# A graph network's last norm: finishing a row in its PSUM bank, and releasing the bank with the sum

## Chip, cores and metric

One core of a Trainium2 chip (trn2). The time is the device time of the whole program, in microseconds; lower is better. The engines are PE (matrix products), DVE (vector), ACT (activations), POOL (here it issues the indirect DMAs) and SP (here it issues the plain DMAs).

## What is computed

Two graph layers over 100,000 nodes with 32 features and 50,000 edges sorted by their end node. The first is a spline convolution, the second an attention layer with 8 heads, both with residuals. For this text only the end of the second layer counts:

```
h  = layer_norm(gat_conv(h, edges) + h, g1, be1)
ff = relu(h @ w1 + b1) @ w2 + b2
x  = x + (layer_norm(ff + h, g2, be2))        # (v - mean) * rsqrt(var + eps) * g2 + be2
```

Everything is fp32.

## The kernel before

Nodes are kept as 125 partitions by 800 slots of 32 features. A unit of work is 125 x 512: 16 slots. The centring of the norms is folded into the matrices (`center`), so a product leaves already centred rows in a PSUM bank; what is left of a norm is the square (ACT, `square`, L921), the sum over 32 features (DVE, `spread`, L1231), the root (ACT, L926), the reciprocal (DVE, `scale_of`, L1236) and the product with it.

Stages, as they follow each other in the queue of every engine, written out by hand:

- A, to about 770 us: spline layer; POOL gathers rows of x (L428).
- B, 25 chunks, two half-turns each: POOL scatters the 25 chunks of new rows (L450, released by L1462 of DVE, semaphore `x1_ready`) and gathers the rows for later chunks between them. Beside each chunk, plain nodes ("units") pass through the whole second layer in three steps n1, n2, n3 in successive half-turns. Seven units are started in ten half-turns, at half-turns 0, 1, 3, 4, 6, 7 and 9 (`UNIT_AT`). Edge rows go through steps e1 to e4.
- D, 25 turns: POOL gathers from the new table (L428, `x_table`); three units in five turns, and from turn 13 on the attention sums of two edge blocks.
- E, 25 rows in five blocks: the rows with edges are finished (`y_finish`) and POOL scatters each to the output, 16 indirect DMAs a row (L476).

`finish_rows` ends n3 in B (35 times) and D (15 times) and every row in E (25 times). It reads the bank that `back_product` on PE has filled with the centred sum of the feed-forward and its input.

The C banks: there are two in B and D and one in E (`cq.depth`). PE fills them in turn. Before it fills one it waits until `c_done` has counted the release of the bank's previous use (`cq.room`). In B the order of fills in a half-turn is n2, e3 or e4, n3, e1 or e2, n1, as far as the step is present; in D it is n2, d2, d1, n3, n1, then the sums of x_early. A `step(...)` on DVE is an instruction that signals a semaphore, and a wait for it behind it: the result is in place before the next instruction starts.

```
def product(cols_T, right, n=GF, bias=None, plus=None, t_at=None, frees=None):
    at, bank = cq.next()
    pe.wait_ge(c_done, cq.room)
```

Of the kernel before, what the change touches and what calls it, by code (L numbers as in the profile page):

```python
# [30 lines left out]
N, E, F, H, HID, KS = 100000, 50000, 32, 8, 128, 9  # L31
P = 125
TN = N // P
NB, NJ, CE = 5, 5, 16
# [15 lines left out]
NU, ND = len(UNIT_AT), len(UNIT_AT_D)  # L50
SLOTS = NU + ND
assert NB * SLOTS * CE == TN and SLOTS == 2 * NJ
CREDIT = 4
# [54 lines left out]
def turn(h, first=False, last=False):  # L108

    at = node_stages(UNIT_AT, HALVES, h)  # L110
    for stage, lag in ((("e3", 1), ("e1", 0)) if h % 2 == 0 else (("e4", 1), ("e2", 0))):
        at[stage] = ((h // 2 - lag) % NJ, h // 2 < lag)
    return {stage: (n, back) for stage, (n, back) in at.items() if not (first and back or last and not back)}


def gnn_program(nc, x, src, dst, edge_attr, w0, root_w, root_b, w_gat, att_src, att_dst, bias_gat,
# [10 lines left out]
    with ExitStack() as ctx:  # L127
# [55 lines left out]
        g2_b = sb("g2_b", [128, F]); be2_b = sb("be2_b", [128, F])  # L183
# [67 lines left out]
        unit = lambda t, k: t[0:P, k, :]  # L251
# [885 lines left out]
        def _(dve):  # L1137
            v = nc.vector
            steps = Uses()
            R = NB * P  # L1140
            tq, cq, vq, nq, rq = Uses(2), Uses(2), Uses(4), Uses(), Uses(2)
            slots = lambda a: a.rearrange("p (s f) -> p s f", f=F)
            wide = lambda a: a.unsqueeze(2).to_broadcast([P, CE, F])

            def step(i):

                at, _ = steps.next()
                i.then_inc(dve_step, 1)
                dve.wait_ge(dve_step, at + 1)
# [84 lines left out]
            def scale_of(k, at):  # L1234
                dve.wait_ge(std_ready, at + 1)
                step(v.reciprocal(unit(rstd, k), unit(std, k)))  # L1236

            def bank_ready():
                at, bank = cq.next()
                dve.wait_ge(c_ready, at + 1)  # L1240
                return at, C[bank][0:P, :]
# [8 lines left out]
            def rows_over_std(k, at):  # L1250
                at_c, rows = bank_ready()
                scale_of(k, at)
                v.tensor_tensor(slots(unit(hrow, k)), slots(rows), wide(unit(rstd, k)), ALU.mult).then_inc(c_done, 1)  # L1253
                return at_c
# [124 lines left out]
            for _ in range(0, 2 * NB, 4):  # L1379
                at, _ = tq.next()  # L1380
# [6 lines left out]
            at, _ = tq.next()  # L1387
# [8 lines left out]

            def finish_rows(x1_part, to, at, signal):

                at_c = rows_over_std(3, at)
                v.tensor_tensor(slots(x1_part), slots(x1_part), be2_b[0:P, :].unsqueeze(1).to_broadcast([P, CE, F]), ALU.add)  # L1400
                dve.wait_ge(c_done, at_c + 1 + CREDIT)
                step(v.tensor_tensor(slots(unit(hrow, 3)), slots(unit(hrow, 3)), g2_b[0:P, :].unsqueeze(1).to_broadcast([P, CE, F]), ALU.mult))
                v.tensor_tensor(to, x1_part, unit(hrow, 3), ALU.add).then_inc(signal, 1)  # L1403


            heads_of = lambda a: a[0:P, :].rearrange("p (h t) -> p h t", h=H)
# [59 lines left out]
            for h in range(HALVES):  # L1466
                b_turn(0, turn(h, first=True))
            steps.restart(); cq.restart()
            STEPS = 4 * NU + NJ * (1 + 5 + 1 + 2)
            with dve.Fori(0, NB - 1) as b:  # L1470
                cq.loop(b, B_USES["c"]); nq.loop(b, B_USES["n"]); steps.loop(b, STEPS)
                for h in range(HALVES):
                    b_turn(b + 1, turn(h))
                cq.end(NB - 1, B_USES["c"]); nq.end(NB - 1, B_USES["n"]); steps.end(NB - 1, STEPS)
            for h in range(2):
# [151 lines left out]
            for b in range(NB):  # L1627
                for w in range(NJ):
                    d_turn(b, w, first=b + w == 0)
                    at = b * NJ + w  # L1630
# [147 lines left out]
```

## Time and profile before

| | |
|---|---|
| median of 3 runs | 3327.99 us (3320.49 to 3328.42) |
| the profiled execution | 3314.93 us, its span 3313.1 us |
| PE busy | 2241.8 us (68%) |
| DVE busy | 1858.4 us (56%) |
| ACT busy | 841.2 us (25%) |
| POOL busy | 2543.9 us (77%) |
| mean granted clock of PE | 0.785 |

Busy shares are means over stages with different limits. A line number in a row is the line in the kernel before. "[1.08 <-DVE hrow L1253]" at the end of a row is the time that the engine stood idle before the instruction, and what ended it; "issue" there means that nothing in the profile explains the idle time.

### The profile page before, as it was taken

What the parts mean: (1) busy time and instruction counts of PE and PEld (TensorE: products, weight loads), DVE (VectorE), ACT (ScalarE), POOL (GpSimd) and SP (SyncE); (2) the same over time, 40 slices, a digit from 0 to 9 for tenths busy, and PEclk for the clock granted to TensorE, in tenths of its full rate; (3) what the DMA queues carried; (4) which work ended last, traced back from release to release, by engine and by line L of the source; (5) the groups of instructions that cost most, each with busy time, mean ns of one, the idle gap of its engine ahead of it and who ended that gap; (6) DMA issues with size and microseconds to landing.
All of it is one profiled execution on the core that took longest, in us unless ns stands there. A gap on an engine that the chain in (4) does not pass through costs nothing.

```text
span 3313.1 us, 33504 instructions
## 1 busy us (share of the span) xinstructions
PE 2241.8 (68%) x10666; PEld 1571.2 (47%) x10666; DVE 1858.4 (56%) x3250; ACT 841.2 (25%) x1614; POOL 2543.9 (77%) x2011
## 2 busy tenths in 40 slices
PE   2877777757777777777777645737767557888730
PEld 1554544535555655565555434534444334455420
DVE  4787988894443433434333313347767578989610
ACT  1332222212323232333323212322222212222210
POOL 7788888888787888788888788888883166888877
PEclk9888888877878787887777766767888668888755
DMA  2322232221212111212111111111110101111100
GB/s 58 87 67 67 68 73 69 55 65 26 39 29 39 38 39 32 43 38 42 36 36 29 28 12 31 24 18 28 21 24 9 44 16 23 33 29 32 28 10 10
DMA packets 116212, 123.93 MB, mean 37 GB/s; under 512 B 70726, under 2 KB 72747, under 8 KB 116070
## 3 DMA queue, kind: packets, MB, share of 16 engines
q0 software_dynamic: 64000, 30.57, 9.9%
q1 hardware_dynamic: 52070, 91.52, 8.7%
q8 instruction: 82, 1.34, 0.2%
q14 instruction: 60, 0.49, 0.0%
HBM read 59.51 MB, written 64.00 MB: 37 GB/s over the span
## 4 chain that ended last, share of the span: by engine, by line
POOL 62%; issue 18%; DVE 9%; PE 9%; ACT 1%; DMA 0%; POOLq 0%; DVEq 0%; ACTq 0%
POOL ring L428 38%; POOL x_table L450 15%; POOL out_rows L476 9%; DVE region L1591 2%; PE V L793 2%; PE C L544 2%; PE V L532 1%; DVE region L1583 1%; PE C L508 1%; DVE region L1262 1%; PE T L493 1%; DVE region L1573 1%; DVE var L1231 1%; PE C L538 1%; PE C L540 0%
## 5 line engine op out<-in xcount | busy, mean ns | idle before, releaser
L428 POOL DMA_INDIRECT ring<-in_x,index x800 | 1040.4, 1300 | 244.3 <-issue 244.0
L476 POOL DMA_INDIRECT out_rows<-ring,index_out x400 | 518.8, 1297 | 272.3 <-DVE ring L1403 152.0
L1231 DVE TENSOR_REDUCE var<-sq 125x16 f32<-125x512 f32 x325 | 220.8, 682 | 802.3 <-ACT sq L921 672.1
L428 POOL DMA_INDIRECT ring<-x_table,index x400 | 495.8, 1240 | 127.0 <-issue 127.0
L450 POOL DMA_INDIRECT x_table<-region,index_out x400 | 485.9, 1215 | 121.9 <-issue 121.9
L532 PE MATMUL V<-xT,w_q 128*128 128x500 f32 x600 | 363.3, 756 | 90.0 <-ACT hid L932 56.5
L921 ACT ACTIVATE sq<-C 125x512 f32<-125x512 f32 x300 | 179.2, 598 | 912.3 <-PE C L544 422.7
L544 PEld LDWEIGHTS C<-w_c,hid 128*125 128x125 f32 x2400 | 317.0, 217 | 0.0
L544 PE MATMUL C<-w_c,hid 128*125 128x32 f32 x2400 | 316.0, 295 | 0.0
L508 PE MATMUL C<-center,xT 128*125 128x128 f32 x1400 | 243.8, 333 | 104.6 <-DVE hrow L1253 61.7
L493 PE MATMUL T<-ident,hrow 125*128 125x125 f32 x1000 | 188.9, 326 | 167.6 <-DVE hrow L1247 137.0
L508 PEld LDWEIGHTS C<-center,xT 128*125 128x125 f32 x1400 | 223.3, 239 | 149.2 <-issue 74.1
L532 PEld LDWEIGHTS V<-xT,w_q 128*128 128x128 f32 x600 | 141.7, 251 | 269.5 <-issue 128.5
L566 PE MATMUL V<-region,hT 128*125 128x384 f32 x600 | 254.2, 539 | 18.3 <-DVE region L1326 17.2
L493 PEld LDWEIGHTS T<-ident,hrow 125*128 125x128 f32 x1000 | 143.3, 171 | 210.1 <-DVE hrow L1247 115.7
L913 ACT ACTIVATE hT<-T 128x500 f32<-128x500 f32 x250 | 146.5, 588 | 373.6 <-PE T L493 315.3
L932 ACT ACTIVATE hid<-V,cols 128x500 f32<-128x500 f32 x300 | 190.6, 679 | 102.2 <-PE V L532 96.7
L493 PE MATMUL T<-ident,ring 125*128 125x125 f32 x300 | 60.3, 337 | 223.4 <-DMA ring<-in_x,index 119.9
L1334 DVE TENSOR_REDUCE region<-region 125x128 f32<-125x1152 f32 x100 | 210.9, 2111 | 0.0
L1326 DVE TENSOR_TENSOR region<-V,region 125x384 f32<-125x384 f32 x300 | 155.7, 551 | 74.4 <-PE V L566 63.9
L1591 DVE TENSOR_REDUCE region<-region 125x128 f32<-125x1024 f32 x100 | 187.8, 1898 | 0.0
L793 PE MATMUL V<-gat_bd,hT 128*125 128x512 f32 x280 | 158.8, 700 | 16.4 <-DVE region L1583 13.6
(248 smaller groups left out, 3207.6 us busy)
## 6 DMA issues: line engine op xcount, KB each, us to landing
ring<-in_x,index POOLq DMA_INDIRECT x800
nodes<-in_x SPq DMA_DIRECT2D x25, 500.0 KB
x_table<-nodes SPq DMA_DIRECT2D x25, 500.0 KB
x_plain<-nodes SPq DMA_DIRECT2D x25, 500.0 KB
nodes<-x_plain SPq DMA_DIRECT2D x50, 250.0 KB
out_rows<-nodes SPq DMA_DIRECT2D x50, 250.0 KB
x_table<-region,index_out POOLq DMA_INDIRECT x400
ring<-x_table,index POOLq DMA_INDIRECT x400
```

Of the source, the lines that this page charges most:

```text
L428: pool.indirect_dma_start(out=ring[0:P, j, s * F:(s + 1) * F], out_offset=None, in_=table, in_offset=bass.IndirectOffsetOnAxis(ap=index[0: ...
L450: pool.indirect_dma_start(out=x1_table[:, :], out_offset=bass.IndirectOffsetOnAxis(ap=index_out[0:P, j, s:s + 1], axis=0), in_=rows_out[0: ...
L476: pool.indirect_dma_start(out=out[:, :], out_offset=bass.IndirectOffsetOnAxis(ap=index_out[0:P, j, s:s + 1], axis=0), in_=ring[0:P, j, s * ...
L493: i = nc.tensor.transpose(T[bank][:, g * P:(g + 1) * P], rows[:, g * GF:(g + 1) * GF], ident[0:P, 0:P])
L508: i = mm(C[bank][0:P, g * n:(g + 1) * n], cols_T[:, g * P:(g + 1) * P], right, start=bias is None and plus is None, stop=True, skip_group_ ...
L532: mm(V[4 - fq.depth + bank][:, 0:WT], w1_q[:, t, :], nT, start=True, stop=True).then_inc(f_ready, 1)
L544: i = mm(C[bank][0:P, (4 * g + t) * F:(4 * g + t + 1) * F], hid[:, t, g * P:(g + 1) * P], w2_c[:, :], start=False, stop=True, skip_group_c ...
L566: mm(V[bank][0:P, 0:3 * GF], hT[:, HE[j], g * P:(g + 1) * P], w0_bd[:, q * 3 * GF:(q + 1) * 3 * GF], start=True, stop=True).then_inc(v_rea ...
L793: mm(banks[bank][0:P, :], hT[:, k, g * P:(g + 1) * P], gat_bd[:, q * 512:(q + 1) * 512], start=True, stop=True).then_inc(v_ready, 1)
L1231: v.tensor_reduce(unit(var, k), slots(squares(k)), AX.X, ALU.add).then_inc(var_ready, 1)
L1334: v.tensor_reduce(msgs[0:P, bass.ds(cv * W + g * GF, GF)], products[0:P, (g % 2) * KS * GF:(g % 2 + 1) * KS * GF].rearrange("p (k c) -> p ...
L1591: v.tensor_reduce(diff[0:P, c * W + g * GF:c * W + (g + 1) * GF], weighted[0:P, (g % 2) * H * GF:(g % 2 + 1) * H * GF].rearrange("p (h c) ...
```

## The change

`finish_rows` applies the reciprocal deviation and the weight g2 in place in the C bank, one after the other, and adds the old row from there. The tile `hrow` 3 is no longer written by it. The addition of the bias be2 to the old row comes first. The bank is released by the last sum, no longer by the product with the reciprocal deviation; the signal to SP or POOL (`signal`) is no longer attached to the sum but is given by a separate instruction behind a wait for the sum. The number of steps in a block of the loop is adapted.

```diff
             def finish_rows(x1_part, to, at, signal):
 
-                at_c = rows_over_std(3, at)
+                _, rows = bank_ready()
+                scale_of(3, at)
                 v.tensor_tensor(slots(x1_part), slots(x1_part), be2_b[0:P, :].unsqueeze(1).to_broadcast([P, CE, F]), ALU.add)
-                dve.wait_ge(c_done, at_c + 1 + CREDIT)
-                step(v.tensor_tensor(slots(unit(hrow, 3)), slots(unit(hrow, 3)), g2_b[0:P, :].unsqueeze(1).to_broadcast([P, CE, F]), ALU.mult))
-                v.tensor_tensor(to, x1_part, unit(hrow, 3), ALU.add).then_inc(signal, 1)
+                step(v.tensor_tensor(slots(rows), slots(rows), wide(unit(rstd, 3)), ALU.mult))
+                step(v.tensor_tensor(slots(rows), slots(rows), g2_b[0:P, :].unsqueeze(1).to_broadcast([P, CE, F]), ALU.mult))
+                v.tensor_tensor(to, rows, x1_part, ALU.add).then_inc(c_done, 1)
+                dve.wait_ge(c_done, cq.at + 1 + CREDIT)
+                dve.sem_inc(signal, 1)
...
-            STEPS = 4 * NU + NJ * (1 + 5 + 1 + 2)
+            STEPS = 5 * NU + NJ * (1 + 5 + 1 + 2)
```

## Rows read from the trace of the kernel before

**Rows 1.** The page's chain by engine and costliest group, and POOL's waits (total, times, longest).

```profile
POOL 62%; issue 18%; DVE 9%; PE 9%; ACT 1%; DMA 0%; POOLq 0%; DVEq 0%; ACTq 0%
...
L428 POOL DMA_INDIRECT ring<-in_x,index x800 | 1040.4, 1300 | 244.3 <-issue 244.0
...
POOL out_rows L476 <- DVE ring L1403: 152.0, 5, 115.8
```

**Rows 2.** Windows, stage B: length, busy PE, PEld, DVE, ACT, POOL, clock, DMA, GB/s.

```profile
795.00:1895.00 1100.00, 823.16 (x4140) 627.18 (x4140) 429.88 (x816) 326.76 (x651) 880.33 (x720) 0.80 0.19 36
```

**Rows 3.** Timeline, one half-turn of B: start, duration, engine, line, operation, output, inputs.

```profile
1332.55 1.12 PE L508 MATMUL C<-center,xT 128*125 128x128 f32 x8
...
1335.46 0.69 DVE L1253 TENSOR_TENSOR hrow<-C,rstd 125x512 f32<-125x512 f32 x1
...
1336.29 2.06 PE L508 MATMUL C<-center,xT 128*125 128x128 f32 x8 [2.62 <-DVE hrow L1253]
1336.67 0.68 DVE L1402 TENSOR_TENSOR hrow<-hrow,g_b 125x512 f32<-125x512 f32 x1
...
1337.39 0.69 DVE L1403 TENSOR_TENSOR nodes<-nodes,hrow 125x512 f32<-125x512 f32 x1
1338.00 0.24 DVE L1236 RECIPROCAL rstd<-std 125x16 f32<-125x16 f32 x1
...
1341.18 1.09 PE L493 MATMUL T<-ident,hrow 125*128 125x125 f32 x4 [2.83 <-DVE hrow L1247]
```

**Rows 4.** Timeline, end of B: last chunk ready, first of its scatters.

```profile
1861.69 0.17 DVE L1462 COPY index_out<-scatter_to 125x16 int32 x1
...
1872.31 1.20 POOL L450 DMA_INDIRECT x_table<-region,index_out  x1 [0.30 <-issue]
```

**Rows 5.** Timeline, first finished row of stage E.

```profile
2633.14 0.69 DVE L1403 TENSOR_TENSOR ring<-nodes,hrow 125x512 f32<-125x512 f32 x1
...
2634.80 2.43 POOL L476 DMA_INDIRECT out_rows<-ring,index_out  x1 [115.77 <-DVE ring L1403]
```

**Rows 6.** Timeline, PE: first gathered chunk of D, and the last that it waits for.

```profile
1927.20 1.07 PE L493 MATMUL T<-ident,ring 125*128 125x125 f32 x4 [38.46 <-issue]
...
2197.44 0.65 PE L493 MATMUL T<-ident,ring 125*128 125x125 f32 x4 [1.48 <-DMA ring<-x_table,index]
```

**Rows 7.** Groups by form (mean ns), and one line's instructions (ns min/median/max).

```profile
L1253 DVE TENSOR_TENSOR hrow<-C,rstd 125x512 f32<-125x512 f32 x125 | 86.4, 691 | 4.3
L1402 DVE TENSOR_TENSOR hrow<-hrow,g_b 125x512 f32<-125x512 f32 x75 | 51.4, 685 | 0.0
...
L1403 DVE TENSOR_TENSOR nodes<-nodes,hrow x50: 691/691/766, 796.3 to 2594.3; 125x512 f32<-125x512 f32 x50
```

**Rows 8.** Timeline, first and last n1 product behind an n3, of 19.

```profile
817.03 1.14 PE L508 MATMUL C<-center,xT 128*125 128x128 f32 x8 [1.08 <-DVE hrow L1253]
...
1858.56 0.69 DVE L1253 TENSOR_TENSOR hrow<-C,rstd 125x512 f32<-125x512 f32 x1
...
1859.38 1.58 PE L508 MATMUL C<-center,xT 128*125 128x128 f32 x8
```

**Rows 9.** Timeline, stage D, DVE's first product behind a finish.

```profile
2440.74 0.69 DVE L1583 TENSOR_TENSOR region<-V,region 125x512 f32<-125x512 f32 x1 [0.98 <-PE V L793]
```

**Rows 10.** Timeline, stage E, from POOL's last long stop.

```profile
2803.11 0.69 DVE L1253 TENSOR_TENSOR hrow<-C,rstd 125x512 f32<-125x512 f32 x1
...
2806.65 1.19 POOL L476 DMA_INDIRECT out_rows<-ring,index_out  x1 [20.31 <-DVE ring L1403]
...
2823.24 0.69 DVE L1253 TENSOR_TENSOR hrow<-C,rstd 125x512 f32<-125x512 f32 x1
...
2830.98 1.70 POOL L476 DMA_INDIRECT out_rows<-ring,index_out  x1 [0.30 <-issue]
...
2918.17 0.69 DVE L1403 TENSOR_TENSOR ring<-nodes,hrow 125x512 f32<-125x512 f32 x1
...
2934.89 1.19 POOL L476 DMA_INDIRECT out_rows<-ring,index_out  x1 [0.31 <-issue]
```

## The prediction

> **What bounds the kernel now.** I read the page first. PE, the busiest compute engine by share, and POOL are both far from idle, but the chain that ended last is POOL's for 62% of the span, and nearly all of it is the issuing of indirect DMAs [rows 1]. So the next question is where POOL stands still. The waits of POOL show only five real stops, 152.0 us in all, and all five lie in the last stage, where POOL scatters finished rows and waits for the sum L1403 [rows 1]. Everywhere else it goes from one DMA to the next with 0.3 us between. An edit that touches DVE, the C banks and PE can therefore cost something in two ways: it moves one of these stops, or it makes some stage so late that POOL gets a new stop. For the second the reader has to look at how much time there is between "data ready" and "POOL takes it", stage by stage.
>
> Three stages hold `finish_rows`: stage B (about 768 to 1894 us, 35 finishes), stage D (to 2595, 15) and stage E (from 2597, 25).
>
> Stage B is not paced by POOL. PE has no wait for a gather there, and DVE is busy 430 us of 1100 [rows 2]. It is one long chain that hands a row from PE to ACT to DVE and back, half-turn by half-turn. One half-turn is in [rows 3]: DVE reads the bank of the finished row (L1253, 1335.46), PE waited 2.62 us for exactly that and starts the n1 product 0.83 us later (1336.29), then comes ACT's square, DVE's reduce, the root and the reciprocal, and the next half-turn's transpose at 1341.18, again after a wait of 2.83 us. In the trace each of these links starts within a tenth of a microsecond or so of the end of the one before, plus the time that a signal takes.
>
> **Where B meets POOL.** Each of its 25 chunks ends in L1462, which releases 16 scatters. The last chunk is ready at 1861.69 and its first scatter starts at 1872.31 [rows 4]. DVE to POOL takes some time: L1403 at 2633.14 is written by 2633.83 and the scatter starts at 2634.80 [rows 5], about 1.0 us. So the last chunk could be at most 1872.31 - (1861.86 + 1.0), about 9.5 us, later before POOL stops. The chunks before it have more cover, the next to last the least of them, some 37 us. After the last scatters POOL goes on to the gathers of stage D; PE waits 38.46 us for the first of them, until 1927.20 [rows 6]. So when the last scatter is late, D is late by the same amount.
>
> **The change, part by part.**
>
> (1) *Length of the finish on DVE.* Before, L1402 starts 1.21 us after L1253 with L1400 between them, L1403 0.72 after that and the next instruction 0.61 after L1403 [rows 3]: 0.6 where an operation doesn't need the one before it, 0.72 where it does. After: the bias add, +0.61 the product with rstd, +0.72 the product with g2, +0.72 the sum. The sum starts 2.05 us after the first of the four, before 1.93: +0.12. Then DVE waits for its own sum before it signals, so the next instruction comes at about +0.74 instead of +0.61. In E `y_finish` has a wait of this kind already, but now there are two in a row. I take +0.25 us a finish in both. The number of wide operations stays four.
>
> (2) *Price of PSUM as an operand.* No DVE write to PSUM is in the trace. The nearest rows: 691 ns with a PSUM source (L1253), 685 with none (L1402) [rows 7]. Lower end 0; upper end the spread of one form, 691 to 766 ns in L1403 [rows 7], so 0.075 us on three operations, 0.23 a finish. I take 0, being nearest to the 6 ns that a PSUM source shows. With 18 finishes on the path (below) and six more in E the upper end is 24 x 0.23 = 5.5 us.
> The Trainium skill (VectorE: DVE Perf Modes, section on the TRN2 errata) speaks against this change: its table gives a fixed 120 cycles for a PSUM source against 58 for SBUF, at 0.96 GHz 65 ns more for each of the two operations that now read PSUM. The trace doesn't bear this out (6 ns). By that rule my sum would be about 3 us higher.
>
> (3) *Release of the C bank.* This is the part that counts. Before, the bank was free when L1253 had read it; now it is free when the sum has read it, whose start is 2.05 us later than L1253's was. Who waits for that? The banks go round two by two. In B, PE fills them in the order n2, e3 or e4, n3, e1 or e2, n1, so in a half-turn with both n3 and n1 the n1 product needs the bank of n3. Units start at half-turns 0, 1, 3, 4, 6, 7, 9 and n3 is two later, so the two meet in half-turns 1, 3, 6 and 9. In the trace I find 19 such meetings, the first with its product at 817.03, the last at 1859.38 [rows 8]. In all of them the n1 product starts 0.74 to 0.98 us after the start of L1253: either it waits for it, or e2's product happens to end at that moment. So it will start 2.05 + 0.74 - (0.74 to 0.98) later: 1.81 to 2.05, mean 1.95, and the square, the reduce and the next transposes move by that less 0 to 0.16 us by which DVE was the later one. I take 1.93. In the half-turns with n3 and no n1 (2, 5, 8) the bank is wanted again only in the next half-turn, whose first work is transposes and the hidden layer: nothing.
> Before x1_ready of the last chunk lie 18 of the 19: 18 x 1.93 = 34.7 us, + 0.1 for its own finish. Less the cover of 9.5: POOL stops for **25.3 us** before the last scatters, and all of D moves by that. The chunk before keeps about 2 us of its 37. The bounds: if only half of each shift comes through, 17.4 - 9.5 = 8; if all of 2.05 does, 36.9 + 0.1 - 9.5 = 27.5.
>
> (4) *Stage D.* Here the n1 product takes d1's bank, not n3's, and until 2197 PE waits for gathers anyway (1.48 us at 2197.44 [rows 6]). After that, three of nine finishes (n3 with n1) have the next reduce right behind them, 0.25 each; behind the others DVE waits for PE, as 0.98 us at 2440.74 [rows 9], and that hides it. +0.8 us; if nothing were hidden, 9 x 0.25 = 2.3.
>
> (5) *Stage E up to POOL's last stop.* Until 2806.65 POOL waits for rows again and again; six finishes lie on that path: 6 x 0.25 = **1.5 us**. The bank isn't missed here: PE needs it only long after.
>
> (6) *Stage E from 2806.65.* One bank only. A wave goes from L1253 at 2803.11 to L1253 at 2823.24, 20.1 us, and PE's product for the finished row starts on that release, so it is a loop between DVE and PE. The release costs up to 2.05 us a wave, so 22.2 us. POOL needs 24.3 us a row (2806.65 to 2830.98), and the next row is ready around 2826, five us ahead. After one block the row whose L1403 starts at 2918.17 is taken at 2934.89, about 16 ahead, and four late releases cost it 7 to 8 [rows 10]. So POOL stays the bound and this costs 0. Were the cover gone, it would be 2 us a wave.
>
> Nothing moves past SP's or POOL's queues; the store of a unit is signalled 0.25 us later. Queued behind DVE's new wait are e1's relu or e2's sum, which the n1 chain outlasts by 2 us.
>
> **Sum.** 25.3 + 0.8 + 1.5 = 27.6 us. Against the profiled execution, 3314.93, that makes 3342.5. It is 13 us faster than the median of the runs shown, 3327.99. I put the sum on the median: **3355.5 us**.
>
> **Rivals.**
> *A, hidden.* The release is late, but B takes it up elsewhere or POOL's cover is larger in most executions: the 13 us between profile and median may be POOL time in A or B, and that would be cover. With 13 more it costs 27.6 - 13 = 15; only when less than 9.5 us comes through of 34.7 is it 0 + 2.3, 3330. Against it: in [rows 3] no link has slack. 0.11 for "within 0.3%", 0.13 for +10 to +19.
> *B, the clock.* In the next half-turn PE stands 2 us longer 19 times. The granted clock in B is 0.80 [rows 2], between the two levels of 1.2 and 2.4 GHz, and the same eight matmuls of L508 take 1.12 us at 1332.55 and 2.06 at 1336.29 behind the wait [rows 3]. If each stop makes one more such group slow, +0.94 x 18 = 17 us: 3372; two groups 3389. For it: the slow groups do stand behind waits. Against it: many stand there slow already. 0.15.
> *C, faster.* POOL's own instructions get shorter because DVE now writes PSUM and not SBUF. The mean of L428 is 1300 ns [rows 1], while a scatter without a stretch takes 1.20 (at 1872.31 [rows 4]). Over 800 gathers that is some 80 us of excess; a third of it would have to go to outweigh the 27.6 us, 38 us of it to be faster by a measurable amount. But DVE writes two tiles less out of many, and no row ties the two. At half the excess it would be 3355.5 - 40 = 3316. 0.03.
>
> **How the numbers follow.** The forecast (+20 to +36) gets 0.58. What a measurement can tell from no change is 0.3%, 10 us. Slower: 0.58 + 0.13 + 0.15 = 0.86; same 0.11; faster 0.03. The low end leaves out A's hidden case and C, 14 in 100: 3328 + 10 = 3338. The high end takes in one slow group a stop and leaves out the rest, some 5 in 100: 3380.
>
> **What would show it.** In B, the n1 product should start some 2.8 us after the start of the rstd product's old place, and x1_ready of the last chunk should stand 35 us further from the first. POOL should show one new stop of about 25 us before L450's last 16 scatters. The wave in E should go from 20.1 to about 22 us without a new stop of POOL, whose last big stop ends about 28 us later. DVE rows of the three operations on C should read 0.68 to 0.70. I am wrong if the last scatters still start without a stop; then half-turns in B didn't get longer, or had cover that I took for a chain.

## The result, and the profile after

The changed kernel took 3353.26 us (median of 4 runs, 3352.15 to 3357.59) against 3326.64 us (4 runs, 3320.49 to 3328.42): ratio 1.0093, 95% interval 1.0071 to 1.0115. It is slower by 26.6 us. Run again later beside 23 runs of the kernel before, it took 3356.6 us (5 runs) against 3321.73: ratio 1.0103, 1.0089 to 1.0118, so 34.9 us. The profiled execution of after is 3352.15 us, the one of before was 3314.93 us. These two traces differ by 37.2 us, more than the first two medians do, and the account below is an account of traces.

In after, L1401 is the bias add, L1402 and L1403 are the two products in the bank, L1404 is the sum, L1406 the separate signal and L1465 the copy that releases the scatters (before: L1462).

The chain of the page, and the waits of POOL (us in total, times, longest), to be held against [rows 1]:

```profile
PE 33%; POOL 27%; DVE 21%; issue 11%; ACT 6%; DMA 0%; DVEq 0%; ACTq 0%; POOLq 0%
...
POOL out_rows L476 <- DVEq L1406: 161.4, 7, 115.7
...
POOL x_table L450 <- DVE index_out L1465: 42.1, 3, 21.4
```

POOL was 62% of the chain; now the hand-over of rows between PE, DVE and ACT is 60% of it. The last line is new: three stops ahead of scatters in stage B (6.2, 14.5 and 21.4 us), which had none. At the output scatters there are 7 waits, before 5. One of the five was only 0.3 us, the usual distance between two DMAs, so three stops have come there: 3.1 us at 2697.6, and the 2.0 and 3.8 us shown below.

The timeline of the changed kernel, one half-turn of B with n3 and n1, the counterpart of [rows 3]:

```profile
1364.91 0.69 DVE L1401 TENSOR_TENSOR nodes<-nodes,be_b 125x512 f32<-125x512 f32 x1
1365.52 0.69 DVE L1402 TENSOR_TENSOR C<-C,rstd 125x512 f32<-125x512 f32 x1
1366.24 0.70 DVE L1403 TENSOR_TENSOR C<-C,g_b 125x512 f32<-125x512 f32 x1
1366.98 0.69 DVE L1404 TENSOR_TENSOR nodes<-C,nodes 125x512 f32<-125x512 f32 x1
...
1367.80 2.07 PE L508 MATMUL C<-center,xT 128*125 128x128 f32 x8 [4.44 <-DVE nodes L1404]
1367.89 0.25 DVE L1236 RECIPROCAL rstd<-std 125x16 f32<-125x16 f32 x1 [0.22 <-DVE nodes L1404]
```

The sum starts 2.07 us after the first of the four, and the n1 product follows the sum by 0.82 us. So the product starts 2.89 us after the place where the rstd product used to start, and PE stood for 4.44 us. PE's waits, as one group:

```profile
PE C L508 <- DVE nodes L1404: 54.7, 19, 4.4
```

Nineteen times, the count of the meetings that the prediction listed [rows 8]. The end of B, the first gather of D and the last wait for one, against [rows 4] and [rows 6]:

```profile
1863.24 1.20 POOL L450 DMA_INDIRECT x_table<-region,index_out  x1 [14.48 <-DVE index_out L1465]
...
1907.24 0.16 DVE L1465 COPY index_out<-scatter_to 125x16 int32 x1
...
1908.35 1.19 POOL L450 DMA_INDIRECT x_table<-region,index_out  x1 [21.40 <-DVE index_out L1465]
...
1934.68 1.24 POOL L428 DMA_INDIRECT ring<-x_table,index  x1 [2.75 <-issue]
...
2229.23 0.65 PE L493 MATMUL T<-ident,ring 125*128 125x125 f32 x4 [1.66 <-DMA ring<-x_table,index]
```

The last chunk is ready 45.6 us later than before (1861.69), and its first scatter starts 36.0 us later: the difference is the 9.5 us of cover. From ready to scatter it is now 1.1 us, so nothing is between them but the signal. The end of D's gathering has moved by 31.8 us (2197.44 before), and so D adds nothing. (The first gather of D has moved by 33.1 us and not by 36.0, because POOL stands 2.75 us ahead of it and stood 5.35 us in the trace of before.) In stage E:

```profile
2840.17 0.69 DVE L1404 TENSOR_TENSOR ring<-C,nodes 125x512 f32<-125x512 f32 x1
...
2840.91 2.07 PE L538 MATMUL C<-bias_row,ones 128*125 128x512 f32 x2 [3.99 <-DVE ring L1404]
...
2841.85 1.19 POOL L476 DMA_INDIRECT out_rows<-ring,index_out  x1 [20.38 <-DVEq L1406]
...
2863.89 0.69 DVE L1404 TENSOR_TENSOR ring<-C,nodes 125x512 f32<-125x512 f32 x1
...
2971.41 1.19 POOL L476 DMA_INDIRECT out_rows<-ring,index_out  x1 [2.01 <-DVEq L1406]
...
3101.10 1.19 POOL L476 DMA_INDIRECT out_rows<-ring,index_out  x1 [3.79 <-DVEq L1406]
```

A wave goes from sum to sum in 23.7 us (20.1 before, [rows 10]), and POOL gets two short stops. The product for the next row takes 2.07 us behind its wait of 3.99; in the trace of before the same one took

```profile
2803.86 1.12 PE L538 MATMUL C<-bias_row,ones 128*125 128x512 f32 x2 [1.92 <-DVE hrow L1253]
```

so it has gone from the upper to the lower of PE's two levels (2.4 and 1.2 GHz) beside waiting longer: the granted clock over these two products is 1.00 before and 0.50 after.

The operands in the bank, by line (ns min/median/max):

```profile
L1402 DVE TENSOR_TENSOR C<-C,rstd x75: 684/692/693, 795.6 to 3278.7; 125x512 f32<-125x512 f32 x75
...
L1403 DVE TENSOR_TENSOR C<-C,g_b x75: 698/700/700, 796.3 to 3279.4; 125x512 f32<-125x512 f32 x75
...
L1404 DVE TENSOR_TENSOR nodes<-C,nodes x50: 690/691/692, 797.1 to 2626.0; 125x512 f32<-125x512 f32 x50
```

The product with g2 takes 700 ns from PSUM to PSUM, and 685 before in SBUF. The other two take what they took before, to 1 ns [rows 7].

**One reading that sorts all the traces.** Stage B is a chain through PE, ACT and DVE. From the x1_ready of its first chunk to that of its last, take the window row (length, then busy time of PE, PEld, DVE, ACT, POOL, clock, DMA share, GB/s) and subtract PE's busy time. The rows of before and of after:

```profile
768.05:1861.69 1093.64, 823.04 (x4141) 628.21 (x4139) 427.92 (x811) 327.72 (x653) 875.57 (x716) 0.80 0.19 36
```
```profile
768.69:1907.24 1138.55, 834.76 (x4136) 635.86 (x4135) 436.71 (x811) 326.78 (x652) 877.80 (x724) 0.78 0.18 35
```

1093.6 - 823.0 = 270.6 us in which PE did nothing, and 1138.6 - 834.8 = 303.8. So of the 44.9 us by which B grew, 33.2 are PE standing and 11.7 are PE being slower at the same work. The same two numbers for every kernel that was run. "(E)" after a name means that the finish is late or longer in E too. "Cover" is how long the last chunk was ready before POOL wanted it, negative if POOL stopped. "Traced" is the time of the one execution from which B, PE busy and cover are read, and "median" is that of all runs; "before" is the median of the kernel before in the same set of runs. All are in us. In two kernels "PE busy" holds added products that nothing uses (76.7 and 38.3 us, see below); without PE's own work alone their B is 320.2 and 300.1 us, so their third number isn't to be held against the others.

| kernel | B | PE busy | without it | cover | traced | median | before | ratio, 95% |
|---|---|---|---|---|---|---|---|---|
| before | 1093.6 | 823.0 | 270.6 | 9.5 | 3314.9 | | | |
| after | 1138.6 | 834.8 | 303.8 | -21 | 3352.2 | 3353.3 | 3326.6 | 1.0093, 1.0071 to 1.0115 |
| after, again | 1142.6 | 837.8 | 304.8 | -31 | 3359.1 | 3356.6 | 3321.7 | 1.0103, 1.0089 to 1.0118 |
| late release, old tiles (E) | 1136.0 | 830.0 | 306.0 | -21 | 3356.5 | 3363.0 | 3319.7 | 1.0122, 1.0091 to 1.0154 |
| late in B only | 1124.6 | 819.4 | 305.2 | -18 | 3336.0 | 3354.1 | 3319.7 | 1.0097, 1.0062 to 1.0132 |
| late in E only | 1106.5 | 834.7 | 271.8 | -6 | 3321.8 | 3324.6 | 3319.7 | 1.0009, 0.9985 to 1.0034 |
| long finish (E) | 1132.7 | 847.1 | 285.6 | -28 | 3352.8 | 3352.8 | 3319.7 | 1.0092, 1.0055 to 1.0129 |
| own wait only (E) | 1109.6 | 839.9 | 269.7 | -6 | 3320.4 | 3327.7 | 3321.7 | 1.0025, 1.0011 to 1.0040 |
| late once a block | 1083.5 | 809.5 | 274.0 | 19 | 3325.8 | 3317.5 | 3320.2 | 0.9976, 0.9963 to 0.9989 |
| bias first | 1101.2 | 828.4 | 272.9 | 0 | 3315.6 | 3319.2 | 3320.2 | 0.9984, 0.9969 to 0.9998 |
| after, PE filled (E) | 1113.7 | 870.2 | 243.5 | -18 | 3330.2 | 3341.3 | 3320.2 | 1.0050, 1.0031 to 1.0070 |
| after, n1 first (E) | 1096.8 | 814.1 | 282.7 | -1 | 3319.3 | 3320.6 | 3320.2 | 0.9987, 0.9972 to 1.0003 |
| long finish, PE filled (E) | 1123.3 | 861.4 | 261.8 | -20 | 3339.0 | 3342.6 | 3321.7 | 1.0071, 1.0049 to 1.0093 |
| n1 and bias first | 1055.7 | 813.3 | 242.5 | 47 | 3322.0 | 3318.9 | 3321.7 | 0.9990, 0.9980 to 1.0000 |

The traced execution isn't always a typical one: that of "late in B only" is 18 us under its median, that of "after, PE filled" 11 us, and that of "late once a block" 8 us above. So a row's first four numbers explain its traced time, and its median only roughly.

### The profile page after: what moved, and what is told of

It is laid out like the page before. It is cut to its first block, busy times and chain, and to the rows that moved or that the text cites. A ratio compares the mean times of both kernels' runs of the same rounds, so it can differ in the third digit from the quotient of the medians.

```text
span 3350.3 us, 33607 instructions
## 1 busy us (share of the span) xinstructions
PE 2276.1 (68%) x10666; PEld 1599.0 (48%) x10666; DVE 1872.7 (56%) x3250; ACT 841.2 (25%) x1614; POOL 2533.6 (76%) x2011
## 4 chain that ended last, share of the span: by engine, by line
PE 33%; POOL 27%; DVE 21%; issue 11%; ACT 6%; DMA 0%; DVEq 0%; ACTq 0%; POOLq 0%
POOL ring L428 21%; PE C L544 7%; PE V L532 7%; POOL out_rows L476 6%; PE C L508 5%; PE T L493 3%; DVE region L1594 3%; DVE var L1231 3%; PE V L793 3%; PE C L538 2%; ACT sq L921 2%; PE C L540 2%; ACT hid L932 2%; DVE region L1586 1%; DVE rstd L1236 1%
## 5 line engine op out<-in xcount | busy, mean ns | idle before, releaser
L428 POOL DMA_INDIRECT ring<-in_x,index x800 | 1041.5, 1302 | 244.4 <-issue 244.1
L476 POOL DMA_INDIRECT out_rows<-ring,index_out x400 | 515.1, 1288 | 281.1 <-DVEq L1406 161.4
L428 POOL DMA_INDIRECT ring<-x_table,index x400 | 494.7, 1237 | 124.5 <-issue 124.2
L508 PE MATMUL C<-center,xT 128*125 128x128 f32 x1400 | 242.8, 332 | 141.8 <-DVE nodes L1404 54.7
L544 PEld LDWEIGHTS C<-w_c,hid 128*125 128x125 f32 x2400 | 327.2, 223 | 0.0
L544 PE MATMUL C<-w_c,hid 128*125 128x32 f32 x2400 | 326.1, 300 | 0.0
L538 PE MATMUL C<-bias_row,ones 128*125 128x512 f32 x150 | 111.7, 836 | 126.3 <-DVE hrow L1253 66.8
```

The source lines that it names most:

```text
L428: pool.indirect_dma_start(out=ring[0:P, j, s * F:(s + 1) * F], out_offset=None, in_=table, in_offset=bass.IndirectOffsetOnAxis(ap=index[0: ...
L476: pool.indirect_dma_start(out=out[:, :], out_offset=bass.IndirectOffsetOnAxis(ap=index_out[0:P, j, s:s + 1], axis=0), in_=ring[0:P, j, s * ...
L508: i = mm(C[bank][0:P, g * n:(g + 1) * n], cols_T[:, g * P:(g + 1) * P], right, start=bias is None and plus is None, stop=True, skip_group_ ...
L544: i = mm(C[bank][0:P, (4 * g + t) * F:(4 * g + t + 1) * F], hid[:, t, g * P:(g + 1) * P], w2_c[:, :], start=False, stop=True, skip_group_c ...
```

## The experiments

**Which part of the change costs.** Four kernels, all from the kernel before. The first has the change's release on the old tiles. Only the signals differ:

```diff
-    at_c = rows_over_std(3, at)
+    _, rows = bank_ready()
+    scale_of(3, at)
+    at_s, _ = steps.next()
+    v.tensor_tensor(slots(unit(hrow, 3)), slots(rows), wide(unit(rstd, 3)), ALU.mult).then_inc(dve_step, 1)
...
-    dve.wait_ge(c_done, at_c + 1 + CREDIT)
+    dve.wait_ge(dve_step, at_s + 1)
...
-    v.tensor_tensor(to, x1_part, unit(hrow, 3), ALU.add).then_inc(signal, 1)
+    v.tensor_tensor(to, x1_part, unit(hrow, 3), ALU.add).then_inc(c_done, 1)
+    dve.wait_ge(c_done, cq.at + 1 + CREDIT)
+    dve.sem_inc(signal, 1)
```

> The tiles of the kernel before are kept (the rstd product goes from the bank to hrow, g2 and the sum work on hrow), only the signals are the change's: the bank is released by the sum, and the finished row is signalled by a separate instruction after it. The sum still starts 1.93 us after the rstd product, so the bank is late by 1.93 us and not by 2.05. My theory (late release of the bank): nearly all of the change's cost, +20 to +28 us over the kernel before by the medians, x1_ready of B's last chunk some 40 us (35 to 45) further from the first, a stop of 15 us or more of POOL ahead of the last scatters of B. Rival (PSUM as operand and target of the two products is what costs): this kernel uses PSUM exactly as the kernel before does, so it would be within 5 us of it, and the finishes would not put a stop into POOL.

It took 3363.0 us, 43 more than before and as much as the change or more. The cost is there with no operand moved into PSUM, so the rival of the PSUM operands falls. (The row "own wait only", below, takes out the other thing in which this kernel differs from the one before.) The last chunk was 42.4 us further from the first, as expected; the 43 us of time are more than the 28 that I had as the upper end. The repeat of the changed kernel, made to settle this, had this expectation:

> The changed kernel as it is, beside the next three. The kernel that has only the late release on the tiles of before measured 3363.0 us (before: 3319.7). Theory (the release is all): 3350 to 3368 us, +30 to +43 over before, so above the +26.6 of the first four runs, which had a before with a higher median. Rival (two products in PSUM cost something of their own): 5 us or more above 3363.

3356.6 us, inside the range of the theory. Working in the bank costs nothing that shows. It goes with something small on POOL, which the rival C of the prediction asked for (before, then after, from the pages):

```profile
L476 POOL DMA_INDIRECT out_rows<-ring,index_out x400 | 518.8, 1297 | 272.3 <-DVE ring L1403 152.0 <-issue 120.4
...
L476 POOL DMA_INDIRECT out_rows<-ring,index_out x400 | 515.1, 1288 | 281.1 <-DVEq L1406 161.4 <-issue 119.7
```

In the four traces whose finish works in the bank (after, its repeat, and the changed kernel with PE filled and with n1 first) POOL is busy 2532.2 to 2538.8 us in all, and the mean of L476 is 1282 to 1288 ns. In the ten others it is 2543.3 to 2551.7 us and 1295 to 1307 ns. So POOL's instructions do get shorter, by about 10 us in all. No run was made to test why.

The second kernel has the change's order and length, but on hrow and with the bank released by the rstd product, which now stands behind the bias add:

```diff
-    at_c = rows_over_std(3, at)
+    at_c, rows = bank_ready()
+    scale_of(3, at)
     v.tensor_tensor(slots(x1_part), slots(x1_part), be2_b[0:P, :].unsqueeze(1).to_broadcast([P, CE, F]), ALU.add)
+    v.tensor_tensor(slots(unit(hrow, 3)), slots(rows), wide(unit(rstd, 3)), ALU.mult).then_inc(c_done, 1)
...
-    v.tensor_tensor(to, x1_part, unit(hrow, 3), ALU.add).then_inc(signal, 1)
+    step(v.tensor_tensor(to, x1_part, unit(hrow, 3), ALU.add))
+    dve.sem_inc(signal, 1)
```

> The order and the length of the change's finish (bias add first, then rstd product, g2, sum, a wait for the sum, a separate signal), but on hrow, with the bank released by the rstd product. So the bank is 0.61 us late and not 2.05, and the finish 0.25 us longer. My theory: 18 meetings in B by 0.61 make 11.0 us, by the factor that the changed kernel showed (2.50 instead of 1.93) up to 14.2; less the cover of 9.5 that is +1.5 to +4.7, and E's rows add 1.5 to 3: +3 to +8 us by the medians. POOL's stop ahead of B's last scatters is at most 5 us. Rival (the longer finish with its own wait on DVE is what costs, wherever the bank is released): +15 us or more.

A miss: 3352.8 us, +33 where +3 to +8 stood. Its window row over B:

```profile
771.66:1904.33 1132.67, 847.11 (x4141) 638.26 (x4139) 437.13 (x812) 328.15 (x653) 879.42 (x721) 0.77 0.18 35
```

Without PE's work it is 285.6 us, +15.0, near the 11.0 to 14.2 that were forecast for the bank. But PE needed 847.1 us for the same 4141 instructions, 24.1 more than in the trace of before, at a granted clock of 0.77 against 0.80. From 1000 to 1600 us it was 0.75. In the trace of before it was 0.80 there. So of the 39.1 us by which B grew in this trace 15.0 are waits and 24.1 are PE's clock, which the forecast had left out.

The third and the fourth put the late release (the first kernel's `finish_rows`, with a last argument that turns it on) into one stage alone, here B:

```diff
-    finish_rows(rows, rows, norm["n3"], unit_done)
+    finish_rows(rows, rows, norm["n3"], unit_done, True)
```

> Late release (by the sum, tiles as in the kernel before) in stage B alone; D and E as before. My theory: B carries most of it. Its last chunk is ready some 40 us later, 9.5 of which POOL's cover takes, D and E follow unchanged: +17 to +27 us by the medians, and E's waves stay at 20.1 us. Rival (half of the loss sits in E, where the changed kernel's waves took 23.7 us instead of 20.1): +8 to +14 us.

> Late release in stage E alone; B and D as before. My theory: the waves get 2 to 3.6 us longer (22 to 23.7 us) but POOL needs 24.3 us a row, so it costs 0 to +4 us by the medians, with at most two short new stops of POOL (under 4 us each). Rival (E's waves set the end once they take 23.7 us): 12 to 16 us over the kernel before, with a POOL stop in front of most rows after 2806 us.

Late in B alone: 3354.1 us, +34, above the range of the theory and far above the rival. Late in E alone: 3324.6 us, not to be told from before. So B carries the loss. The traced run of the third is the shortest of its six, at a granted clock of 0.791: PE was busy 819.4 us in B, no more than before, and the 34.6 us without PE's work are there all the same. So the late bank costs by itself, at 3336.0 us some 16 above before; the other runs, up to 3366.1 us, have mean clocks down to 0.780. The trace of the fourth also holds a surprise, since its B is that of the kernel before:

```profile
769.42:1875.89 1106.47, 834.68 (x4141) 637.61 (x4139) 427.72 (x811) 328.14 (x653) 881.46 (x723) 0.79 0.19 35
```
```profile
1876.99 1.20 POOL L450 DMA_INDIRECT x_table<-region,index_out  x1 [6.07 <-DVE index_out L1474]
```

The same code took 12.8 us longer in B, 11.6 of them PE's busy time, and POOL already stopped for 6 us. The cover of 9.5 us on which the forecast rests was that of one execution; in three others whose B should be like before or quicker it is 0, -6 and -6 us.

**Is there cover at all?** The late release only where n3 is unit 3, once in a block:

```diff
-    finish_rows(rows, rows, norm["n3"], unit_done)
+    finish_rows(rows, rows, norm["n3"], unit_done, at["n3"][0] == 3)
```

> The bank is released late (by the sum) at one meeting of each block of stage B only, so 5 meetings in place of 18 ahead of the last x1_ready; the rest as in the kernel before. It asks whether there is cover at all. In two executions with B's unchanged code B took 1093.6 and 1106.5 us, PE was busy 823.0 and 834.7 of them, and what is left is 270.6 and 271.8. With 5 late releases of 1.93 us it should be 280 to 282. My theory now (B's end and POOL's arrival stand so close that most executions have no cover): +6 to +11 us by the medians. Rival (a cover of 9.5 us as in the first trace): 5 x 1.93 = 9.7, less 9.5: 0 to +2 us.

3317.5 us, 2.7 less than before: neither my theory nor quite the rival, and no loss. In the trace the n1 product does stand 4.2 to 4.3 us at these five places, and starts 1.9 us later relative to the finish than in before, but B without PE's time is only 3.4 us longer and PE's work takes 809.5 us, 13.5 less than in before. The finishes of B come in five rounds of seven. In the second, third and fourth round the first five distances between them repeat to 0.1 us (20.8, 45.8, 16.7, 45.6, 18.4 us); in before the fourth distance changes from round to round, 42.8, 50.3, 43.8, 50.4, 49.1 us. I read this as PE being at its one level or its other in the same place of the chain, so that the cost of a delay depends on the pattern of slow and fast groups into which the loop falls after it. No run was made to test that. The cover in this trace is 19 us, so here nothing of a B that is 3.4 us longer could show in the time; that B grew by 3.4 us and not by 9.7 is the part that stays unexplained.

**Does PE lose clock by standing?** The changed kernel, with products whose results nothing uses, computed where PE would wait:

```diff
+    if fill is not None:
+        pe.wait_ge(t_done, t_at + 1 + CREDIT)
+        for _ in range(fill):
+            mm(T[fill_bank[0]][:, 0:WT], w1_q[:, 0, :], cols_T, start=True, stop=True)
...
-    st["n1"] = product(xT[:, 1, :], center[:, :], t_at=t["n1"])
+    st["n1"] = product(xT[:, 1, :], center[:, :], t_at=t["n1"], fill=4 if "n3" in at else None)
```

> The changed kernel, and in each half-turn of B with both n3 and n1, PE computes four products that nothing uses (128 x 500, in the bank of the last transposes) while it would wait for the C bank. It asks whether PE's stops cost clock. Theory of the clock: with PE busy through the stop the n1 product behind it runs at the higher level (1.12 us and not 2.06), PE's own work in B takes less than the 834.8 us of the changed kernel once the added products are taken off, and B gets 5 to 20 us shorter than its 1138.6. Rival (the stop costs only its own length; the clock goes its way): B within 5 us of 1138.6 or, where the added products outlast the stop, longer; time equal to the changed kernel or up to 15 us more.

The window over B, all instructions and then the added ones alone:

```profile
771.68:1885.38 1113.70, 870.21 (x4283) 633.04 (x4282) 437.44 (x811) 326.20 (x652) 876.70 (x723) 0.82 0.19 35
```
```profile
771.68:1885.38 1113.70, 76.69 (x150) 33.15 (x151) 0.82 0.19 35
```

PE's own work is 870.2 - 76.7 = 793.5 us, 41.3 less than in after, at a granted clock of 0.82 against 0.78. B is 24.9 us shorter though PE does more, and the time is 3341.3 us, 12 to 15 less than the two medians of after (+21.1 over the before of its own set, where after has +26.6 and +34.9). The theory holds, with more gain in B than its 20 us. The traced run is one of the shorter ones of its twelve, but the clock doesn't hang on it: all twelve have 0.790 to 0.799, and the nine runs of after 0.778 to 0.785. The added products also outlast the stops, so without PE's own work B is 16.4 us longer (320.2 against 303.8); that and the 41.3 us make the 24.9. Standing at the meetings costs clock, and the clock costs time.

The Trainium skill (TensorE: Matmul & The Clock Gate, section on a second failure mode, cycling through PSUM banks) tells of a kernel whose PE idles shortly between groups and whose clock swings between the two levels. The traces agree: 0.82 where the stops are filled, 0.78 where they are not.

The same test on the kernel with the long finish, with two such products at each meeting (`fill=2`):

> The kernel with the long finish and the bank 0.61 us late (3352.8 us, granted clock 0.780 by the mean of its runs), with two products that nothing uses computed by PE at each meeting of n3 and n1 in B, ahead of the wait for the bank. Theory (its excess over the 3 to 8 us of the late bank is PE at the lower level): the mean clock rises above 0.785, PE's own work in B falls from 847 to under 825 us, and the time to 3322 to 3335 us. Rival (the excess is of another kind): 3345 us or more.

The clock rose as expected (mean of the runs 0.79, without the added products 0.78), and PE's own work fell to 861.4 - 38.3 = 823.1 us. But the time is 3342.6 us, 10 less and not 20 to 30, and with 7 and 6 scattered runs the two ratios (1.0092 and 1.0071) have intervals that overlap. The traces tell why so little is gained. PE's own work is back at the 823 us of before, so all 24 us of excess clock time were given back; but the added products outlast the shorter stops here, and B without PE's own work is some 15 us longer (300.1 against 285.6). That leaves 9.4 us of B.

**DVE's wait for its own sum, alone.**

```diff
-    v.tensor_tensor(to, x1_part, unit(hrow, 3), ALU.add).then_inc(signal, 1)
+    step(v.tensor_tensor(to, x1_part, unit(hrow, 3), ALU.add))
+    dve.sem_inc(signal, 1)
```

> The kernel before, where only the end of a finish changes: the row is signalled by a separate instruction after DVE has waited for its own sum, 0.14 us later. The bank is released as early as before. In the run where the bank came 0.61 us late and DVE had this wait too, B without PE's busy time was 15 us longer than before, of which 18 x 0.61 = 11.0 were the bank's. Theory (the bank and the clock): this one is within 3 us of before, B without PE's busy time under 274. Rival (DVE's wait for itself stretches the chain): B without PE's busy time 275 or more, +4 us or more.

B without PE's time is 269.7 us, as in before, so this wait doesn't stretch the chain. The time, +6 us (1.0025), is above the 3 that I allowed. The mean clock of its twelve runs is 0.782, that of before 0.785; at the 18 us for each 0.01 by which the runs of before differ (last section), that would be about 5 us, an estimate.

**Remedies.** n1 ahead of e1 and e2 on the changed kernel, so that another product meets n3's late bank (the same moves on ACT and DVE):

```diff
+    if "n1" in at:
+        st["n1"] = product(xT[:, 1, :], center[:, :], t_at=t["n1"])
...
-    if "n1" in at:
-        st["n1"] = product(xT[:, 1, :], center[:, :], t_at=t["n1"])
```

> The changed kernel with n1's product, its square and root and its relu moved ahead of e1 and e2 in B, on PE, ACT and DVE: n1 then takes the bank of e3 or e4, which was free long ago, and e1 or e2 takes n3's. My theory (the late bank stretches B only because n1's product stands on it): B without PE's busy time goes from 303.8 back to 275 or less, POOL has no stop over 10 us ahead of the last scatters, and the time is +2 to +12 us over the kernel before (E keeps its share) against +26.6 for the change. Rival (the stretch comes from the longer finish on DVE or from the clock): it stays within 8 us of the changed kernel, 20 us or more over the kernel before.

The whole loss is gone: 3320.6 us, ratio 0.9987, better than the +2 to +12 us expected. Its waits on PE:

```profile
PE C L506 <- DVE nodes L1404: 52.8, 14, 4.0
...
PE C L508 <- DVE nodes L1404: 20.5, 5, 4.5
```

It still stands 19 times for the late bank and for 73.3 us in all, more than the 54.7 of after; 14 of these stops are now before e1's product (L506). B without PE's time is 282.7 us, more than the 275 expected and 21 less than in after. It looks as if the late bank cost little in front of e1's product. The last run below shows that this is not so.

The bias add ahead of the wait for the root, in the kernel before:

```diff
+    v.tensor_tensor(slots(x1_part), slots(x1_part), be2_b[0:P, :].unsqueeze(1).to_broadcast([P, CE, F]), ALU.add)
     at_c = rows_over_std(3, at)
-    v.tensor_tensor(slots(x1_part), slots(x1_part), be2_b[0:P, :].unsqueeze(1).to_broadcast([P, CE, F]), ALU.add)
```

> The kernel before with one line moved: the bias add of the old row ahead of the wait for the root and the rstd product, where DVE has idle time. The bank is released as early as before, and g2's product follows the rstd product by 0.72 us and not 1.21, so each finished row is signalled 0.5 us earlier. Expected: six rows of E on POOL's path by 0.5 make -3 us, B's last chunk 0.5 us earlier: -1 to -6 us by the medians. Rival (DVE's idle time is not there, so the bias add pushes the rstd product and with it the bank): +5 us or more, with the n1 product 0.3 to 0.6 us later in B.

-1.0 us by the medians, ratio 0.9984 with an interval up to 0.9998: at the edge of what was expected and under the 0.3% that count here. And both remedies together:

> The kernel before with both remedies: the old row's bias add ahead of the wait for the root, and n1's chain ahead of e1 and e2 in B; the bank is released early, by the rstd product. Expected: B without PE's busy time at or under 271 us, the last x1_ready 10 us or more ahead of the last scatters, and since POOL sets the end then, -2 to -8 us by the medians. Rival (e1 and e2, now behind n1, become the chain): B without PE's busy time 278 us or more, the time equal to before.

```profile
773.46:1829.20 1055.74, 813.29 (x4135) 609.46 (x4134) 430.88 (x811) 324.92 (x652) 845.42 (x691) 0.80 0.19 37
```

The row of the changed kernel with n1 first, to be held against it:

```profile
776.68:1873.47 1096.79, 814.13 (x4135) 610.10 (x4134) 438.14 (x811) 325.92 (x653) 876.76 (x720) 0.81 0.19 36
```

These two kernels differ in `finish_rows` alone: early release on hrow here, late release in the bank there. In the old order bias first and after differ in the same way. So there are four cases (B without PE's busy time, us, each from one trace):

| | early release | late release |
|---|---|---|
| old order | 272.9 | 303.8 |
| n1 first | 242.5 | 282.7 |

The late release costs 30.9 us in the old order and 40.2 with n1 first, and of B's whole length 37.3 and 41.1 us. So it isn't cheaper in front of e1's product. The new order itself makes B shorter, by 45.5 us with the early release, and that is what pays for the late bank: B of the changed kernel with n1 first ends at 1873.47, where POOL comes for it, with a stop of 1.8 us. The theory of that run, that the late bank stretches B only because n1's product stands on it, has failed.

With both remedies B is 37.9 us shorter than in before, and the last chunk is ready 47.7 us before its first scatter, which starts at 1876.85. The time is 3318.9 us, 2.8 less. In the three traces without a stop (before, late once a block, and this one) POOL reaches these scatters between 1872 and 1877 us. A B that ends earlier only waits for POOL. This is the other side of the change: a B that ends later than about 1871 to 1876 makes POOL wait for it, and that is time.

## Why the prediction was right, step by step

The forecast, 3355.5 us and slower, lies between the two medians of after (3353.3 and 3356.6), and the mechanism is the one it named. Its sum was 27.6 us. Measured: 26.6 and 34.9 us by medians, 37.2 between the two traces. So the sum was somewhat short, and part of the hit is luck of the base: 3327.99 was the median of three runs, while later sets of 18, 35 and 23 runs of the kernel before have medians of 3319.7, 3320.2 and 3321.7. On those the same sum gives 3347 to 3349, which is 4 to 9 us under the two medians.

- *Term 1, length of the finish.* The sum starts 2.07 us after the first operation (forecast 2.05), and the reciprocal behind it follows at +0.91 with a wait of 0.22, where 0.74 stood; the finish is 0.44 us longer than before and not 0.25. DVE's wait for its own sum, alone, leaves B's chain at 269.7 us: no cost on the chain.
- *Term 2, PSUM as operand.* Taken as 0, with an upper end of 75 ns an operation. It is 0 to 15 ns against the same operation before (rstd product 692 and 691, g2 700 and 685, sum 691 and 691), 16 ns a finish, and the kernel without PSUM targets isn't faster than the changed one. The 65 ns that the Trainium skill's errata table (VectorE: DVE Perf Modes) would ask are not seen: the sum with a PSUM source takes 691 ns, the same length as before with none.
- *Term 3, release of the C bank.* 19 meetings, found. Each product starts 2.81 to 2.93 us after the place of the rstd product, where 2.8 stood. Forecast 34.8 us for B; PE stood 33.2 us longer in after, 34.2 in the repeat, 34.6 and 35.4 in the kernels with the late release on old tiles. This was the part worked out from the rows, and it is right to 2 us. The three traces whose B should be that of before lie between 269.7 and 271.8 us without PE's time, so this number, unlike the time itself, is steady enough for one pair.
- *What term 3 left out* is the clock, which stood as rival B: another 11.7 us of PE's busy time in after, 14.8 in the repeat. 33.2 + 11.7 = 44.9, and 0.6 by which B began later, less 9.5 of cover, move the last scatters by 36.0 us and the gathers of D by 33.1, where 25.3 stood. The forecast was one stop, with 2 us of cover left to the chunk before; there were three, the chunk before came 52 us later and cost a stop of 14.5 us. The three make 42.1 us, 6.1 more than the scatters moved: POOL itself got to them that much sooner. The price for rival B (+17) was made from "one more slow group a stop". In after 13 of the 19 n1 products at the meetings took over 1.6 us, in before 5, so eight more and not eighteen. How much of the 11.7 is the change's can't be read from one pair, since the same code gave 823.0 and 834.7 us. That PE's stops cost clock is shown by filling them (-41 us of its own work). That they needn't in every run is shown by the traced run with the late release in B alone, in which PE was busy 3.6 us less than in before.
- *The cover of 9.5 us* was a reading of one execution. Others have 0 and -6, and the kernel with one late release a block has 19, so the size of this term is not fixed: it moves with PE's busy time in B, which is 840 and 835 us in the two traces with -6 and 810 in the one with 19. Rival A supposed more cover in most executions; in three of these four there is less.
- *Terms 4 and 5, D and E up to POOL's last long stop.* From the first gather of D to that stop after takes 907.2 us, before 905.1: +2.1 where 0.8 + 1.5 stood. But kernels with unchanged D and E take 905.1 to 914.8 us there, so these terms can't be told from the spread. Of the "five real stops" of before that the prediction names the fifth was 0.3 us, so there were four.
- *Term 6, E's waves.* The release makes a wave 3.6 us longer and not 2.05. L538 behind the longer wait takes 2.07 us and no longer 1.12, but that is not the reason: with the late release in E alone the waves take 23.7 to 23.8 us too, where L538 takes anything from 2.07 down to 1.39. What makes the rest isn't shown. POOL got stops of 2.01 and 3.79 us where none was expected, and from its last long stop to its last instruction it takes 504.3 us, before 502.3: +2.0 instead of 0. The run with the late release in E alone can't be told from no change. And from the first gather of D to POOL's last instruction, kernels without a late release in E take 1407.4 us (before), 1409.0 (bias first, and late in B only), 1412.9 (n1 and bias first) and 1418.7 (late once a block); the changed one takes 1411.5. The mechanism is seen in the wave, but its price is inside that spread.
- *Rival C, faster.* The gathers on which it was built are no shorter (L428 1302 ns, before 1300), and the kernel isn't faster. But its direction was right: over all its DMAs POOL is some 10 us less busy in the kernels that work in the bank.

**What stays open.** Why PE loses as much clock in the kernel with the long finish, whose bank is only 0.6 us late, as in those with a bank 1.9 us late or more: its trace adds up (15.0 of waits and 24.1 of PE's work, less the cover), but the low clock itself has no cause that a run shows. Why five late releases stretch B by 3.4 us and not by 9.7. How the loss of after, 27 to 35 us, divides between the late bank and the clock in its median run: the traces give about 33 and 12 to 15 before the cover is taken off, and the clock differs from run to run without any change. And why POOL's instructions are shorter when the finish works in the bank.

## What to carry to other kernels

Before you release a buffer later, find out which instruction takes it next, and how much later the stage may end before another engine waits for it. A remedy that brings the time back hasn't for that reason removed the cost: moving the n1 product to another bank left the late bank as dear as before (31 and 40 us of B) and paid for it with a better order. Only the fourth case, the new order with the early release, tells the two apart. A stage that ends close to where another engine picks up its result has a cover that can differ by 15 us and more from one execution to the next, so read it in several traces before you subtract it. And subtract PE's busy time from the length of a stage when you compare traces: what is left shows the waits you made, and what you took off shows the clock.

## What the runs showed of the hardware

- Same code, same 4141 instructions of PE in B: 823.0 us in one execution and 834.7 in another. Over the 35 runs of the kernel before in one set, the granted clock of the whole span lay between 0.780 and 0.791 and went with the time (correlation -0.88, 18 us less for each 0.01).
- More work can be faster: 150 added matmul instructions (76.7 us busy) in PE's stops took 41.3 us off its other work, and the median is 12 us or more lower.
- DVE works in place in PSUM at 692 ns (product with rstd) and 700 ns (product with g2) for 125 x 512 fp32; the latter takes 685 with SBUF alone.
- With the finish in PSUM, POOL is busy 2532 to 2539 us in four traces; with it in SBUF, 2543 to 2552 us in ten.
- From the end of the DVE instruction that releases it to the start of POOL's indirect DMA it takes 0.93 to 0.97 us, in every stop of over 1 us that DVE ended, in all fourteen traces.
